# Pair values of a 27-wide Gram matrix taken along its diagonals: three row chunks in the first layer in place of four, one write per half tile, six reads

## The chip, the cores and the metric

The kernel runs on one core of a Trainium2 chip. The metric is the device time of one execution in microseconds (us), the median of 3 runs, taken without the profiler. In the rows PE is the matrix engine (PEld its weight load), DVE, ACT and POOL are the vector, scalar and GpSimd engines, and SPq, ACTq and POOLq are the queues on which SP, ACT and POOL issue transfers (DMAs).

## The reference

A batch of 512 rows looks up 27 embeddings of 128 numbers, takes the product of every pair of them, appends 16 dense features and runs three layers:

```python
e = jnp.stack([tbl_0[ids[:, 0]], ..., tbl_26[ids[:, 26]]], axis=1)   # 512 x 27 x 128
interactions = jnp.einsum('bnd,bmd->bnm', e, e)
i, j = jnp.triu_indices(27, k=1)
z = interactions[:, i, j]                                            # 512 x 351
h = jnp.concatenate([z, dense_ctx], axis=1)                          # 512 x 367
h = jnp.maximum(h @ W_top1 + b_top1, 0.0)                            # 367 x 512
h = jnp.maximum(h @ W_top2 + b_top2, 0.0)                            # 512 x 256
y = h @ W_top3                                                       # 256 x 1
```

Everything is float32.

## The kernel before

The batch is cut into T = 4 tiles of 128 rows. 15 features come by indirect gathers that POOL issues (L328, one for each feature and tile, and one more for the last tile, 61 in all). PE transposes them in groups of up to four ("quads", numbered 0 to 15, four for each tile, L347), and DVE or ACT copies them into `ET` (L479, L560). The other 12 features, from the smaller tables, are picked by products with a one-hot matrix `hot` (L369), which DVE and ACT build (L500, L586) while SP loads the tables. POOL holds back a gather at six places until DVE has built a certain `hot` (the list `HELD`, L326).

Then `product_unit` (L386) multiplies, for two batch rows at a time, the 27 features with themselves, eight units in all, two for each tile. DVE and ACT copy the results to `gram` (L513, L597). The Gram values lie there with one batch row to a group of partitions, while the first layer wants one pair to a partition. So each tile goes through HBM: SP writes one half and ACT the other, each in two DMAs (`write_last_block` L182, `write_other_blocks` L189), into `pair_blocks`, where each of three blocks holds 9 of the 27 columns. `read_pairs` (L210) reads it back into `zT`, with 128-byte pieces of 32 batch rows. In the blocks the pairs are rectangles, so 459 rows are read for 351 pairs; those of a pair that comes twice meet rows of zeros in the weights. With the 16 dense rows they fill NC = 4 chunks:

```python
CHUNKS = [[(2, 0, 14)], [(1, 0, 14)], [(0, 0, 8), (1, 14, 17)], [(2, 14, 26)]]   # (block, first row, end)
SP_READS = [(0, 1, 2), (0, 1, 2, 3), (0, 1, 2, 3), (0, 2)]                       # chunks by tile
ACT_READS = [(3,), (), (), (1,)]
```

For the last tile chunk 0 and 2 are read by SP, 1 by ACT and 3 by POOL. The first layer (L398 for tiles 1 and 2, which waits for all chunks first; L413 for tiles 0 and 3, which waits chunk by chunk) does four products of 128 columns for each chunk. Each float32 product stands as two records in the trace, so a chunk is 8 records and a layer 32.

The order of the work on PE, DVE and ACT is a list written out by hand, `steps`; each engine walks through it and does its part:

```python
steps = quads(9, 10) + units(0) + [("write", 0), ("unit", U)] + quads(10, 12) + [("unit", U + 1), ("read", 0), ("write", 1)]
steps += units(2) + [("write", 2)] + quads(12, 13) + mlp(0) + quads(13, 14)
steps += [("layer1", 1), ("layer3", 0), ("layer2", 1), ("layer2_end", 1)] + quads(14, 16) + [("layer3", 1)]
steps += units(3) + [("write", 3)]
```

After that come the three layers of tile 2 and those of tile 3. SP goes through the tiles in order: wait for the Gram matrix, write, wait for what was written, read.

## Time and profile before

| | us |
|---|---|
| median of 3 runs without the profiler | 112.94 (112.81 to 113.18) |
| span of the profiled execution | 141.2 |
| PE busy / PE weight load busy | 112.1 / 93.6 |
| DVE / ACT / POOL busy | 73.8 / 70.5 / 68.8 |

The profile gives the span of the execution that it recorded, from the first to the last instruction, and no time of that execution beside it: what lies around the span is not known. The span is 28.3 us longer than the median of the runs without the profiler, so this trace holds waits that those runs don't have, or have shorter. Times in the rows are in the trace's own coordinates, 0 to 141.2.

### The profile page before, as it was taken

How to read it: one execution, taken by the hardware profiler on the slowest of the kernel's cores; microseconds unless marked ns; L12 is line 12 of the kernel's file. 1: busy time of each engine (PE TensorE's matmuls, PEld its weight loads, DVE VectorE, ACT ScalarE, POOL GpSimd, SP SyncE). 2: the span in 40 equal slices, each digit the busy share in tenths (PEclk: the TensorE clock that was granted, in tenths of full speed). 3: DMA queues.
4: the chain of work that ended last, by engine and by line, in shares of the span. 5: the costliest groups of instructions: out<-in, count | busy, mean ns of one | idle time of the engine just before them, and what ended most of it. 6: DMA issues, size and time to landing. Idle time of an engine off the chain costs nothing.

```text
span 141.2 us, 2513 instructions
## 1 busy us (share of the span) xinstructions
PE 112.1 (79%) x1025; PEld 93.6 (66%) x1025; DVE 73.8 (52%) x68; ACT 70.5 (50%) x100; POOL 68.8 (49%) x81
## 2 busy tenths in 40 slices
PE   5969999998999987069994212126999999999894
PEld 5938777775877865047892110105999998899792
DVE  2799999999999980699100000200446212451221
ACT  4099999999999960699440000002255211151021
POOL 2578788887877887147877777740000000002000
PEclk9999999999999999965899555555599999999999
DMA  2896788989768699201112222110037543004300
GB/s 62 292 357 220 239 241 268 267 252 279 170 229 258 150 383 331 61 0 37 48 45 56 60 56 56 44 49 0 14 119 188 118 105 49 0 5 143 54 0 1
DMA packets 15877, 18.74 MB, mean 133 GB/s; under 512 B 9425, under 2 KB 11805, under 8 KB 15738
## 3 DMA queue, kind: packets, MB, share of 16 engines
q1 hardware_dynamic: 11864, 13.39, 32.1%
q0 software_dynamic: 2000, 4.06, 10.2%
q10 hardware_dynamic: 2002, 1.14, 2.8%
q8 instruction: 8, 0.13, 0.4%
q14 instruction: 3, 0.02, 0.0%
HBM read 16.80 MB, written 1.77 MB: 132 GB/s over the span
## 4 chain that ended last, share of the span: by engine, by line
PE 42%; DVE 31%; issue 18%; another core or an unknown queue 4%; DMA 3%; SPq 0%; ACT 0%; DVEq 0%
DVE hot L500 22%; PE psG L386 14%; DVE parts L505 9%; PE psG L369 7%; PE psG L413 5%; PE psH L398 5%; PE psH L429 4%; DMA pick_ids<-in_picked_ids 3%; PE psT L347 3%; PE psG L429 1%; PE psH L444 1%; DVE hot L488 1%; PE psG L444 0%; SPq L264 0%
## 5 line engine op out<-in xcount | busy, mean ns | idle before, releaser
L328 POOL DMA_INDIRECT rows<-in_tbl,ids_sb x61 | 62.9, 1032 | 19.7 <-issue 15.8
L369 PE MATMUL psG<-hot,parts 128*128 128x512 f32 (+1 forms) x216 | 56.1, 410 | 7.7 <-DVE hot L500 6.2
L369 PEld LDWEIGHTS psG<-hot,parts 128*128 128x128 f32 x216 | 40.7, 198 | 19.9 <-DVE hot L500 6.2
L500 DVE TENSOR_TENSOR hot<-pick_ids,psH 128x1536 fp32r<-128x1536 int32 (+2 forms) x23 | 41.6, 1851 | 5.3 <-remote 5.3
L386 PE MATMUL psG<-ET 128*52 128x54 f32 x512 | 20.2, 234 | 17.3 <-issue 17.3
L386 PEld LDWEIGHTS psG<-ET 128*52 128x52 f32 x512 | 17.5, 146 | 20.3 <-issue 19.7
L513 DVE COPY gram<-psG 128x432 f32<-128x432 f32 x8 | 7.2, 903 | 36.0 <-issue 21.3
L597 ACT COPY gram<-psG 128x432 f32<-128x432 f32 x8 | 7.2, 905 | 32.0 <-remote 23.2
L586 ACT ACTIVATE hot<-pick_ids,row_no 128x512 fp32r<-128x512 int32 (+1 forms) x30 | 19.4, 711 | 0.0
L210 POOL DMA_DIRECT2D zT<-pair_blocks x1 | 0.9, 883 | 35.9 <-DMA pair_blocks<-gram 35.9
L505 DVE TENSOR_TENSOR parts<-table,parts 128x1024 fp32r<-128x1024 f32 (+1 forms) x12 | 16.3, 1358 | 0.0
L590 ACT ACTIVATE hot<-hot 128x1024 fp32r<-128x1024 f32 (+2 forms) x12 | 15.0, 1247 | 0.4
L577 ACT CAST parts<-table 128x1280 fp32r<-128x1280 f32 (+1 forms) x11 | 12.8, 1167 | 0.0
L565 ACT COPY ET<-psG 128x512 f32<-128x512 f32 (+1 forms) x12 | 7.5, 622 | 10.0 <-remote 6.1
L560 ACT COPY ET<-psT 128x512 f32<-128x512 f32 (+1 forms) x13 | 7.3, 573 | 4.7 <-PE psT L347 4.7
L347 PE MATMUL psT<-ident,rows 128*128 128x128 f32 x61 | 8.9, 274 | 0.0
L347 PEld LDWEIGHTS psT<-ident,rows 128*128 128x128 f32 x61 | 7.2, 140 | 1.2
L413 PE MATMUL psG<-zT,w_sb 126*128 126x128 f32 (+2 forms) x64 | 7.7, 278 | 0.0
L413 PEld LDWEIGHTS psG<-zT,w_sb 126*128 126x128 f32 (+2 forms) x64 | 7.4, 191 | 0.3 <-issue 0.2
L398 PE MATMUL psH<-zT,w_sb 126*128 126x128 f32 (+2 forms) x64 | 7.6, 276 | 0.0
L398 PEld LDWEIGHTS psH<-zT,w_sb 126*128 126x128 f32 (+2 forms) x64 | 7.3, 191 | 0.1
L449 PE MATMUL psH<-ident 128*128 128x128 f32 x28 | 5.7, 397 | 1.5 <-POOL ident L303 1.5
(35 smaller groups left out, 47.0 us busy)
## 6 DMA issues: line engine op xcount, KB each, us to landing
table<-in_tbl SPq DMA_DIRECT2D x6, 640.0 KB
table<-in_tbl SPq DMA_DIRECT2D x6, 512.0 KB
pick_ids<-in_picked_ids SPq DMA_DIRECT2D x11, 256.0 KB, 3.3
w_sb<-in_w SPq DMA_DIRECT2D x1, 1024.0 KB
rows<-in_tbl,ids_sb POOLq DMA_INDIRECT x61
pair_blocks<-gram ACTq DMA_DIRECT2D x4, 144.0 KB, 2.5
pair_blocks<-gram SPq DMA_DIRECT2D x4, 144.0 KB, 3.5
w_sb<-in_w SPq DMA_DIRECT2D x1, 512.0 KB
```

Of the source, the lines that this page charges most:

```text
L328: pool.indirect_dma_start(out=rows[:, n % RING, x, :], out_offset=None, in_=gathered_tables[f], in_offset=bass.IndirectOffsetOnAxis(ap=ids ...
L347: last = pe.transpose(psT[:, n % 2, x, :], rows[:, n % RING, x, :], ident[:, :])
L369: last = pe.matmul(psP[:, k % 2, 0:looked_up(k)], parts[:, k % 2, x, c, :], hot[:, k % 2, c, 0:looked_up(k)], start=x == 0 and c == 0, sto ...
L386: last = pe.matmul(psG[R * h:R * h + S * J, m % 2, bank, S * F * x:S * F * (x + 1)], group[:, 0:S * J], group, start=True, stop=True)
L398: last = pe.matmul(h1_psum(t, n), w1_sb[0:ROWS[c], c, P * n:P * (n + 1)], zT[0:ROWS[c], t, c, :], start=c == 0, stop=c == NC - 1)
L413: last = pe.matmul(h1_psum(t, n), w1_sb[0:ROWS[c], c, P * n:P * (n + 1)], zT[0:ROWS[c], t, c, :], start=c == 0, stop=c == NC - 1)
L500: dve.tensor_tensor(hot[:, k % 2, first:end, 0:many], pick_ids[:, k % TABLES, 0:many].unsqueeze(1).to_broadcast(shape), numbers.unsqueeze( ...
L505: dve.tensor_tensor(parts[:, k % 2, 1, 0:CH[k], :], table[:, k % TABLES, 0:CH[k], :], parts[:, k % 2, 0, 0:CH[k], :], ALU.subtract).then_i ...
L565: act.copy(ET[:, 0:tiles, :, F - 1 - k, :], psP[:, k % 2, 0:P * tiles].rearrange("d (t s g) -> d t g s", t=tiles, s=S)).then_inc(picked_ou ...
L577: act.copy(parts[:, k % 2, 0, 0:CH[k], :], table[:, k % TABLES, 0:CH[k], :]).then_inc(high_ready, 1)
L586: act.activation(hot[:, k % 2, c, 0:looked_up(k)], pick_ids[:, k % TABLES, 0:looked_up(k)], ACT.Abs, bias=row_number(k, c), scale=-1.0).th ...
L590: act.activation(last, last, ACT.Relu, bias=1.0, scale=-1.0).then_inc(last_hot_ready, 1)
```

## The change

`gram` is written as it lies, all 27 columns of a half tile in one DMA (64 rows of 3,456 bytes, `write_gram`, L182 of the kernel after), into `pair_grams`. There the value of features i and j has the number 27 i + j. Since 27 i + j equals j - i plus a multiple of 28, all numbers 7 m + 1 lie on diagonals j - i of 1, 8, 15, 22 or their like below the main one, and no pair comes twice; the numbers 7 m + 1, 7 m + 2 and 7 m + 3 (104 each), 28 m + 7 (26) and 28 m + 14 (13) hold each of the 351 pairs once. `read_pairs` reads these with a stride, two DMAs for each chunk (104 and 13 rows), six for a tile in place of five. The 16 dense rows go to chunks 0 and 1, 8 each, by two DMAs. The chunks have 125, 125 and 117 rows, where the four had 126, 126, 99 and 124. `w1` is padded to 3 x 128 rows (768 KB) in place of 4 x 128 (1,024 KB). The left operand of a pair product takes all 54 columns in place of 52, since the strided numbers reach into the last feature's row.

```diff
-    J = F - 1
...
-    NB = F // WIDTH
...
-    PAIR_ROWS = [sum(WIDTH * (end - first) for b, first, end in chunk) for chunk in CHUNKS]
-    ROWS = PAIR_ROWS[:NC - 1] + [PAIR_ROWS[NC - 1] + DN]
+    PAIR_ROWS = [sum(end - first for step, offset, first, end in chunk) for chunk in CHUNKS]
+    DENSE_IN = 2
+    DH = DN // DENSE_IN
+    ROWS = [n + (DH if c < DENSE_IN else 0) for c, n in enumerate(PAIR_ROWS)]
...
-    SP_READS = [(0, 1, 2), (0, 1, 2, 3), (0, 1, 2, 3), (0, 2)]
-    ACT_READS = [(3,), (), (), (1,)]
+    SP_READS = [(0, 1), (0, 1, 2), (0, 1, 2), (0,)]
+    ACT_READS = [(2,), (), (), (1,)]
+    POOL_READS = (2,)
...
-        blocks = nc.dram_tensor("pair_blocks", (T, NB, S, G, WIDTH * GH), fp32, kind="Internal").ap()
+        grams = nc.dram_tensor("pair_grams", (T, S, G, F * GH), fp32, kind="Internal").ap()
...
-        def write_last_block(eng, t, s):
-
-            eng.dma_start(blocks[t, NB - 1, s, :, :],
-                          gram[s:P:S, t % 2, s, WIDTH * (NB - 1):F, :].rearrange("q j g -> q (j g)")
-                          ).then_inc(last_block_out[t], 16)
-
-        def write_other_blocks(eng, t, s):
-
-            src = gram[s:P:S, t % 2, s, 0:WIDTH * (NB - 1), :]
-            eng.dma_start(blocks[t, 0:NB - 1, s, :, :].rearrange("b q x -> q b x"),
-                          src.rearrange("q (b j) g -> q b (j g)", b=NB - 1)).then_inc(other_blocks_out[t], 16)
-
-        def wait_block_of(eng, t, c):
-
-            if CHUNKS[c][0][0] == NB - 1:
-                eng.wait_ge(last_block_out[t], 16 * S)
-            else:
-                eng.wait_ge(other_blocks_out[t], 16 * S)
+        def write_gram(eng, t, s):
+
+            eng.dma_start(grams[t, s, :, :], gram[s:P:S, t % 2, s, :, :].rearrange("q j g -> q (j g)")
+                          ).then_inc(gram_out[t], 16)
 
         def wait_written(eng, t):
 
-            eng.wait_ge(last_block_out[t], 16 * S)
-            eng.wait_ge(other_blocks_out[t], 16 * S)
+            eng.wait_ge(gram_out[t], 16 * S)
 
         def read_pairs(eng, t, c):
 
             r = 0
-            for b, first, end in CHUNKS[c]:
-                n = WIDTH * (end - first)
-                src = blocks[t, b, :, :, :].rearrange("s (h i) x -> (s h) i x", h=H)[:, first:end, :]
+            for step, offset, first, end in CHUNKS[c]:
+                n = end - first
+                src = grams[t, :, :, :].rearrange("s (h i) x -> (s h) (i x)", h=H)
+                src = src[:, 0:step * GH * end].rearrange("q (m k g) -> k m q g", k=step, g=GH)
                 eng.dma_start(zT[r:r + n, t, c, :].rearrange("r (q g) -> r q g", q=Q),
-                              src.rearrange("q i (j g) -> (i j) q g", g=GH)).then_inc(chunk_in[t][c], 16)
+                              src[offset, first:end, :, :]).then_inc(chunk_in[t][c], 16)
                 r += n
...
         steps += mlp(2) + [("read", T - 1), ("layer3", T - 2), ("chunk", 0), ("chunk", 1), ("chunk", 2),
-                           ("chunk", 3), ("relu1", T - 1), ("layer2", T - 1), ("layer3", T - 1)]
+                           ("relu1", T - 1), ("layer2", T - 1), ("layer3", T - 1)]
...
-            sp.dma_start(zT[PAIR_ROWS[NC - 1]:ROWS[NC - 1], :, NC - 1, :],
-                         dense_rows.rearrange("k (t p) -> k t p", p=P)).then_inc(dense_in, 16)
+            for c in range(DENSE_IN):
+                sp.dma_start(zT[PAIR_ROWS[c]:ROWS[c], :, c, :],
+                             dense_rows[DH * c:DH * (c + 1), :].rearrange("k (t p) -> k t p", p=P)).then_inc(dense_in, 16)
...
-                write_last_block(sp, t, 0)
-                write_other_blocks(sp, t, 0)
+                write_gram(sp, t, 0)
+                wait_written(sp, t)
                 for c in SP_READS[t]:
-                    wait_block_of(sp, t, c)
                     read_pairs(sp, t, c)
...
-            wait_block_of(pool, T - 1, 3)
-            read_pairs(pool, T - 1, 3)
+            wait_written(pool, T - 1)
+            for c in POOL_READS:
+                read_pairs(pool, T - 1, c)
...
-                            last = pe.matmul(psG[R * h:R * h + S * J, m % 2, bank, S * F * x:S * F * (x + 1)],
-                                             group[:, 0:S * J], group, start=True, stop=True)
+                            last = pe.matmul(psG[R * h:R * h + S * F, m % 2, bank, S * F * x:S * F * (x + 1)],
+                                             group, group, start=True, stop=True)
...
-                    pe.wait_ge(dense_in, 16)
+                    pe.wait_ge(dense_in, 16 * DENSE_IN)
...
-                write_last_block(act, t, 1)
-                write_other_blocks(act, t, 1)
+                write_gram(act, t, 1)
 
             def read_half(t):
+                wait_written(act, t)
                 for c in ACT_READS[t]:
-                    wait_block_of(act, t, c)
                     read_pairs(act, t, c)
...
-        return a * n - a * (a + 1) // 2 + b - a - 1 if i < j else -1
-
-    chunks = [[pair(i, j) for b, first, end in chunk for i in range(first, end)
-               for j in range(WIDTH * b, WIDTH * (b + 1))] for chunk in CHUNKS]
-    chunks[-1] += [n * (n - 1) // 2 + x for x in range(n_dense)]
+        return a * n - a * (a + 1) // 2 + b - a - 1
+
+    chunks = [[pair(*divmod(step * m + offset, n)) for step, offset, first, end in chunk for m in range(first, end)]
+              for chunk in CHUNKS]
+    for c in range(2):
+        chunks[c] += [n * (n - 1) // 2 + x for x in range(n_dense // 2 * c, n_dense // 2 * (c + 1))]
     return [c + [-1] * (128 - len(c)) for c in chunks]
...
 PICKED = 12
-WIDTH = 9
-CHUNKS = [[(2, 0, 14)], [(1, 0, 14)], [(0, 0, 8), (1, 14, 17)], [(2, 14, 26)]]
+CHUNKS = [[(7, 1, 0, 104), (28, 7, 0, 13)], [(7, 2, 0, 104), (28, 7, 13, 26)], [(7, 3, 0, 104), (28, 14, 0, 13)]]
```

On PE, from the units of tile 3 to the last tile's layer 1, these rows stood in the order of the program before (`zT` is the input of layer 1, `chunk_in_t_c` says that chunk c of tile t has landed):

```order
L386 MATMUL psG<-ET 52x54 [waits gram_act]
L386 MATMUL psG<-ET 52x54 x15
L398 MATMUL psH<-zT,w_sb 128x128 [waits chunk_in_2_3,chunk_in_2_2,y_ready,chunk_in_2_1,chunk_in_2_0]
L398 MATMUL psH<-zT,w_sb 128x128 x15
...
L413 MATMUL psG<-zT,w_sb 128x128 [waits chunk_in_3_2]
L413 MATMUL psG<-zT,w_sb 128x128 x3
L413 MATMUL psG<-zT,w_sb 128x128 [waits chunk_in_3_3]
L413 MATMUL psG<-zT,w_sb 128x128 x3
L429 MATMUL psH<-h,w_sb 128x128 [waits h1_dve]
```

and these stand there now:

```order
L373 MATMUL psG<-ET 54x54 [waits gram_act]
L373 MATMUL psG<-ET 54x54 x15
L385 MATMUL psH<-zT,w_sb 128x128 [waits chunk_in_2_2,y_ready,chunk_in_2_1,chunk_in_2_0]
L385 MATMUL psH<-zT,w_sb 128x128 x11
...
L400 MATMUL psG<-zT,w_sb 128x128 [waits chunk_in_3_2]
L400 MATMUL psG<-zT,w_sb 128x128 x3
L416 MATMUL psH<-h,w_sb 128x128 [waits h1_dve]
```

Four products, 8 records, are gone from each tile's layer 1, and nothing else moved on PE. On SP's queue these rows stood for tile 3 before:

```order
L182 DMA pair_blocks<-gram 64x288 [waits gram_act,gram_dve]
L189 DMA pair_blocks<-gram 64x2x288
L210 DMA zT<-pair_blocks 126x4x32 [waits last_block_out_3]
L210 DMA zT<-pair_blocks 72x4x32 [waits other_blocks_out_3]
L210 DMA zT<-pair_blocks 27x4x32
```

and these now:

```order
L182 DMA pair_grams<-gram 64x864 [waits gram_act,gram_dve]
L196 DMA zT<-pair_grams 104x4x32 [waits gram_out_3]
L196 DMA zT<-pair_grams 13x4x32
```

The first read no longer starts when a third of the tile is written: it waits for all of it. POOL's queue ended before with one read, and ends now with two, of the chunk that layer 1 takes last:

```order
L196 DMA zT<-pair_grams 104x4x32 [waits gram_out_3]
L196 DMA zT<-pair_grams 13x4x32
```

ACT reads chunk 1 of tile 3 and chunk 2 of tile 0, each with such a pair of rows in place of one.

## Rows read from the trace of the kernel before

**Rows 1.** The page: busy time by engine.

```profile
span 141.2 us, 2513 instructions
PE 112.1 (79%) x1025; PEld 93.6 (66%) x1025; DVE 73.8 (52%) x68; ACT 70.5 (50%) x100; POOL 68.8 (49%) x81
```

**Rows 2.** Stages: PE, PEld, DVE, ACT, POOL busy (instructions), granted clock, DMA share, GB/s.

```profile
52.50:57.70 5.20, 3.27 (x17) 2.48 (x15) 0.01 (x1) 0.00 (x0) 3.66 (x4) 1.00 0.91 290
...
73.40:97.10 23.70, 6.56 (x72) 4.19 (x71) 0.88 (x1) 0.80 (x2) 15.26 (x17) 0.60 0.18 48
```

**Rows 3.** Chain that ended last, in order of time: start, us, what.

```profile
52.51 5.21 another core or an unknown queue
...
61.82 6.99 PE psG L369 x17
...
125.92 3.77 PE psH L398 x32
```

**Rows 4.** Timeline, PE and POOL: start, us, operation, idle before it.

```profile
51.16 4.17 PE L369 MATMUL psG<-hot,parts 128*128 128x512 f32 x17 [0.42 <-DVE hot L500]
...
62.34 1.65 POOL L328 DMA_INDIRECT rows<-in_tbl,ids_sb  x1
...
66.80 1.52 POOL L328 DMA_INDIRECT rows<-in_tbl,ids_sb  x1 [0.30 <-issue]
...
92.59 0.94 POOL L328 DMA_INDIRECT rows<-in_tbl,ids_sb  x1 [0.30 <-issue]
...
97.08 5.48 PE L386 MATMUL psG<-ET 128*52 128x54 f32 x123 [0.37 <-issue]
...
103.41 4.88 PE L386 MATMUL psG<-ET 128*52 128x54 f32 x192
...
120.84 1.04 PE L347 MATMUL psT<-ident,rows 128*128 128x128 f32 x8
```

**Rows 5.** The same stages' view after the last gather's issue.

```profile
94.80:96.00 1.20, 0.56 (x2) 0.16 (x1) 0.00 (x0) 0.00 (x0) 0.00 (x0) 0.50 0.00 0
```

**Rows 6.** Groups by line and shape: count, busy us, mean ns, idle before.

```profile
L413 PE MATMUL psG<-zT,w_sb 126*128 126x128 f32 x32 | 4.1, 282 | 0.0
...
L413 PE MATMUL psG<-zT,w_sb 99*128 99x128 f32 x16 | 2.1, 275 | 0.0
```

**Rows 7.** Timeline, tiles 0 and 1 on SP's queue.

```profile
101.09 0.53 SPq L182 DMA_DIRECT2D pair_blocks<-gram  x1
...
104.84 1.85 SPq L210 DMA_DIRECT2D zT<-pair_blocks  x4
...
110.52 2.15 SPq L210 DMA_DIRECT2D zT<-pair_blocks  x5
```

**Rows 8.** Timeline, tile 3, all engines and queues.

```profile
126.06 0.91 ACT L597 COPY gram<-psG 128x432 f32<-128x432 f32 x1 [0.65 <-PE psG L386]
127.03 0.46 SPq L182 DMA_DIRECT2D pair_blocks<-gram  x1
...
129.16 1.73 SPq L210 DMA_DIRECT2D zT<-pair_blocks  x3
...
129.43 0.88 POOL L210 DMA_DIRECT2D zT<-pair_blocks  x1 [35.90 <-DMA pair_blocks<-gram]
...
130.18 0.35 ACTq L210 DMA_DIRECT2D zT<-pair_blocks  x1
...
132.85 3.65 PEld L413 LDWEIGHTS psG<-zT,w_sb 126*128 126x128 f32 x32 [0.22 <-issue]
```

**Rows 9.** POOL's read of tile 3, from issue to landing.

```profile
DMA to landing us min/median/max: 2.9/2.9/2.9
```

**Rows 10.** Windows while the reads of tile 3 land.

```profile
131.00:132.00 1.00, 0.79 (x8) 0.60 (x6) 0.17 (x1) 0.00 (x0) 0.00 (x0) 1.00 0.90 145
132.00:133.00 1.00, 0.68 (x5) 0.40 (x6) 0.48 (x3) 0.00 (x0) 0.00 (x0) 1.00 0.18 27
```

**Rows 11.** Windows while the weights load.

```profile
50.00:52.00 2.00, 1.58 (x8) 0.99 (x7) 2.00 (x2) 1.60 (x2) 1.69 (x3) 1.00 1.05 413
```

More of the change, by code:

```diff
@@ L166, in dlrm_tower @@
         gram_act = sem("gram_act")
-        last_block_out = [sem(f"last_block_out_{t}") for t in range(T)]
-        other_blocks_out = [sem(f"other_blocks_out_{t}") for t in range(T)]
+        gram_out = [sem(f"gram_out_{t}") for t in range(T)]
         chunk_in = [[sem(f"chunk_in_{t}_{c}") for c in range(NC)] for t in range(T)]
```

## Prediction

> **What bounds the kernel now.** I begin with the page's first rows: no engine is busy for the whole span, PE comes nearest with 79% [rows 1]. So the bound changes from stage to stage, and the windows and the chain that ended last have to say where. Two stages stand out. In one of 5.2 us DVE and ACT are idle while the DMA engines are at 0.91 of their time; the chain gives 5.21 us there to "another core or an unknown queue". In one of 23.7 us PE has 72 records at a mean granted clock of 0.60, between its two levels of 1.2 and 2.4 GHz [rows 2, 3]. The rows show no tile and no engine that it waits for. The runs without the profiler take 112.94 us, 28.3 less than the span, and these two stages are the only ones large enough to hold that. So I rebuild the time without them. The first three units and the transposes of quad 9 end at 102.56, after 29.1 us from 73.40; the same 192 records of the next three units took 4.88 us: 24.3 us less. The 5.2 us stall goes. After it, with PE just out of its idle time, 17 pick products took 6.99 us, where 17 had taken 4.17 before it: 2.8 us less. 141.2 - 24.3 - 5.2 - 2.8 = 108.9 [rows 2 to 4]. The median is 4.0 us above, which I count as what lies around the span. The sum below is one of differences, and I take them off the 112.94.
>
> In this rebuilt time two chains meet at quad 15, the last to be transposed. PE's own chain (picks, units, layers of tiles 0 and 1) reaches it, halfway through the eight transposes at 120.84, so at about 121.4 in the trace, and at 121.4 - 32.3 = 89.1 in the rebuilt time. POOL issues the last gather at 92.59, and the DMA engines are idle from 94.8 on. POOL was held up by the stall alone, since it waited for a `hot` of DVE's, so its data are there at 94.8 - 5.2 = 89.6, or 1.3 us sooner (88.3) if its two long issues (1.65 and 1.52 against 0.94) belong to the stall too [rows 4, 5]. That is even within a microsecond, so work that PE loses before quad 15 may be worth nothing. Behind quad 15 PE is the chain: units of tile 3, layer 1 of tile 2, layer 1 of tile 3, with no wait for a transfer in the rows; the weight load is idle for 0.22 us ahead of the last layer 1 [rows 8].
>
> **The change, part by part.**
>
> *Four products, 8 records, less in each layer 1.* A layer of 32 records takes 3.77 us, so a chunk is 3.77 / 4 = 0.94 us. That the chunk holds fewer or more rows doesn't matter: records of 99 rows take 275 ns, of 126 rows 282 [rows 3, 6]. So -0.94 for each of four tiles: two after quad 15 (-1.88) and two ahead of it (-1.88 at most).
>
> *54 columns in place of 52 on the left.* 192 records in 4.88 us are 25.4 ns each [rows 4]. No row has 54 columns. Lower bound 0 (the 54 columns that stream by are the same), upper bound in proportion, 25.4 x 2/52 = 1.0 ns: 0.13 us for the 128 records after quad 15, 0.38 for the 384 ahead. I take the upper ones, since weight loads fill this stage as much as products do.
>
> The Trainium skill (TensorE: Matmul & The Clock Gate, LDWEIGHTS) says that a weight load takes its columns divided by 1.2 ns, whatever the number of rows. By that a left operand of 54 costs 1.7 ns more than one of 52, an estimate of 0.21 us after quad 15 in place of 0.13, and the sum would be 0.08 us less gain. On the number of rows the trace agrees (275 against 282 ns).
>
> *Ahead of quad 15.* PE gains at most 1.88 - 0.38 = 1.5 us there. The other bound is 0, if the gathers come at 89.6 or later. The rows put PE between 0.5 us ahead of the data and 0.8 behind (89.1 against 89.6 and 88.3). Such slack, plus an error of half a microsecond in a rebuilt time, is what can be gained; I take 0.6 us. Tile 1's reads could bind first: SP issues six reads there in place of five, at 2.15 / 5 = 0.43 each, while the write is one issue of about 0.5 in place of two, and so the last read goes out at about the same time, against a PE that comes 0.94 sooner [rows 7]. That stays inside the 0.6.
>
> *The write, tile 3.* Before, `gram` was ready at 126.97, SP issued at 127.03, the smaller write was seen landed at 129.16 (2.1 us), and both at 130.18 (3.15 us), of which the second issue cost 0.5 [rows 8]. Now one DMA holds all. No row shows a write of 3,456 bytes a row. Lower bound 2.1, as the smaller write; upper bound 3.75, as tile 0 had it (101.09 to 104.84) [rows 7]. I take 2.6, the full one without the second issue: all written at 129.65.
>
> *The reads, tile 3.* SP's second read for chunk 0 goes out 0.43 later, at 130.1. What a read takes on SP's queue is not in a row of its own. POOL's took 2.9, with 0.88 of issue; SP had issued its last by 130.89, and the DMA share falls from 0.90 to 0.18 after 132 [rows 8 to 10]. So the estimate is 1.5 to 2.5; I take 2.0: chunk 0 is in at 132.1. PE, 0.94 sooner, wants it at 132.85 - 0.94 = 131.9. So it waits 0.2, where it waited for nothing. Chunk 1 (ACT, the same times) is wanted 0.94 later. Chunk 2 is POOL's now, by two reads: 129.65, then 0.88 of issue and the 0.30 that lies between POOL's issues, and from 130.83 another 2.9: 133.7. It is wanted at 132.1 + 1.88 = 134.0. So it is just hidden, and 0.3 later it isn't. Behind POOL's reads nothing is queued; ACT's two reads stand ahead of its activations of tile 3, which can't come before the layer 1 that starts at 132.85 has done its last chunk, and cost nothing while that cover of more than 2 us lasts.
>
> *The rest.* `w1` is 256 KB smaller. At 413 GB/s [rows 11] that is 0.6 us less of transfer in the stage of full DMA. In the rebuilt time nothing waits there, so 0; if the 5.2 us stall hangs on those transfers and is partly there without the profiler, up to -0.6. One more small DMA for the dense rows is issued on SP long ahead of its use: 0.
>
> Sum: -1.88 + 0.13 + 0.2 - 0.6 = -2.15, and 112.94 - 2.15 = **110.8 us**.
>
> The Trainium skill (DMA: Bandwidth & Descriptors, Rules for kernel authors) speaks against this side of the change: many small transfers should be one large one, since under 64 KB one pays mostly overhead. All the new reads are under that, and there is one more in a tile. The trace shows the overhead as issue time, 0.43 us a read; by the rule, the second read of a chunk costs as much issue as the first, and with that the sum comes out at the same 2.15 us.
>
> **The rivals.** *(A) The gathers don't bind.* Then all that is gained ahead of quad 15 counts: -1.88 + 0.13 + 0.2 - 1.5 = -3.05: 109.9, and with the smaller `w1` 109.3. For it: the order of `steps` puts quads 14 and 15 as late as it can, and the rebuilt slack may be short by a microsecond. Against it: POOL issues without a pause to the end, and the numbers meet.
>
> *(B) The exchange of tile 3 becomes the bound.* If the write takes 3.75, it has landed at 130.78, chunk 0 is in at 133.2 and PE waits 1.3 us in place of 0.2; POOL's last chunk then comes at 134.9, against a want of 135.1, so nothing is added. The gain is 1.88 - 0.13 - 1.3 = 0.45 us and what was gained ahead, 0.6: 111.9. For it: tiles 0 and 1 show such slow writes. Against it: tile 3's was fast, with no other traffic beside it.
>
> *(C) The strided reads are slow: no gain, or slower.* A 104-row read takes every seventh 128-byte piece, where the blocks gave 9 in a row. The old pieces filled a window at 0.90 share and 145 GB/s; a tile's 351 x 512 bytes = 180 KB at 145 / 0.9 = 161 GB/s take 1.1 us [rows 10]. At three times the time for a piece the reads end 2.2 us later; the wait of 0.2 becomes 2.4, tile 1's reads bind too and nothing is gained ahead: -1.88 + 0.13 + 2.4 = +0.65: 113.6. The point from which it decides is a wait of 1.75 us. For it: nothing in the rows shows a strided read. Against it: the pieces are as long as before, and 24% fewer.
>
> **How the numbers follow.** The forecast has 0.52, (A) 0.24, (B) 0.14, (C) 0.10. The likeliest case has its own range: 0 to 1.2 us ahead of quad 15 and a wait of 0 to 0.7 give 110.0 to 111.9. The range goes to both neighbours, down to (A) with the smaller `w1` and up past (B): 109.3 to 112.1. 0.3% is 0.34 us, about what a measurement of this kernel can tell from no change. (C) is shared between same and slower; a small part of (B) lies in "same": faster 0.87, same 0.06, slower 0.07.
>
> **What the profile after would show.** Layer 1 has 24 records in place of 32 and takes 2.8 us. The pair products have 54 columns and 192 records take 4.9 to 5.1 us. In tile 3 the first read is issued 2.6 us after the write, and PE is idle for 0.4 us or less ahead of the last layer 1. POOL's two reads start about 1.2 us apart and PE doesn't wait for chunk 2. If the slow stage of the units is there again, the gathers have landed long before quad 15, so the trace itself may show up to 3 us from quad 9 to the end where the runs without the profiler gain 2. An idle PE ahead of L400 of a microsecond or more is (B) or (C), told apart by when the first read is issued. Gains near 3 us in the runs are (A). What would make the prediction wrong above all is the rebuilt time: that the gathers and PE meet at quad 15 is worked out, not seen.

## The result and the profile after

The kernel after takes 111.98 us (median of 12 runs, 111.23 to 112.3), the kernel before 113.02 beside it (12 runs, 111.94 to 114.38): a ratio of 0.9914 (0.9887 to 0.9941), 0.97 us less (0.7 to 1.3). Ratios, here and below, leave disturbed executions out, so they differ somewhat from the quotient of the medians where these scatter, and the three profiles that are of such executions have a * in the tables. The direction is as forecast and the time lies in the range, near its upper end and just above the 110.0 to 111.9 of the likeliest case, but the gain is less than half of the 2.15 forecast. The profiled execution of the kernel after took 111.96 us with a span of 109.8, so 2.2 us lie around the span.

The page of the kernel after, its span, busy times, granted clock by slice and chain:

```profile
span 109.8 us, 2437 instructions
PE 99.7 (91%) x993; PEld 84.2 (77%) x993; DVE 73.7 (67%) x68; ACT 70.5 (64%) x100; POOL 69.1 (63%) x82
...
PEclk9999999999999999999999999999999999999999
...
POOL 37%; DVE 24%; issue 14%; DMA 12%; PE 9%; ACT 1%; SPq 1%; POOLq 0%; ACTq 0%
```

Neither of the two stages of [rows 2] is here. They are no work of the profiler's, as the prediction had it: of the five chips used below, three gave the kernel before 112.7 to 112.9 us without the profiler, and two 143.2 to 143.3. Each chip was used once, so the runs don't tell whether it is the chip or the hour; "of the first kind" and "of the second kind" below mean no more than these two times. So a clean trace of the kernel before is needed, and one taken on a chip of the first kind (span 110.4) stands here. From its PE timeline, the units on (start, us, operation, idle before it):

```profile
65.53 4.88 PE L386 MATMUL psG<-ET 128*52 128x54 f32 x192
70.34 0.98 PE L347 MATMUL psT<-ident,rows 128*128 128x128 f32 x7
71.25 4.88 PE L386 MATMUL psG<-ET 128*52 128x54 f32 x192
76.06 0.66 PE L347 MATMUL psT<-ident,rows 128*128 128x128 f32 x4
77.99 3.81 PE L413 MATMUL psG<-zT,w_sb 126*128 126x128 f32 x32 [1.27 <-DMA zT<-pair_blocks]
...
83.96 3.74 PE L398 MATMUL psH<-zT,w_sb 126*128 126x128 f32 x32
...
90.04 1.04 PE L347 MATMUL psT<-ident,rows 128*128 128x128 f32 x8
91.01 0.60 PE L444 MATMUL psH<-h,w_sb 128*1 128x128 f32 x4
91.80 3.32 PE L386 MATMUL psG<-ET 128*52 128x54 f32 x128 [0.20 <-issue]
95.06 3.84 PE L398 MATMUL psH<-zT,w_sb 126*128 126x128 f32 x32
...
102.05 3.84 PE L413 MATMUL psG<-zT,w_sb 126*128 126x128 f32 x32
...
107.66 0.91 PE L444 MATMUL psH<-h,w_sb 128*1 128x128 f32 x4
```

The same view of the kernel after:

```profile
65.31 5.12 PE L373 MATMUL psG<-ET 128*54 128x54 f32 x192
...
71.27 3.05 PE L373 MATMUL psG<-ET 128*54 128x54 f32 x113
75.28 2.21 PE L373 MATMUL psG<-ET 128*54 128x54 f32 x79 [0.95 <-issue]
...
77.91 2.92 PE L400 MATMUL psG<-zT,w_sb 125*128 125x128 f32 x24
...
84.26 2.92 PE L385 MATMUL psH<-zT,w_sb 125*128 125x128 f32 x24 [1.10 <-DMA zT<-pair_grams]
...
89.53 0.60 PE L334 MATMUL psT<-ident,rows 128*128 128x128 f32 x4
91.19 0.66 PE L334 MATMUL psT<-ident,rows 128*128 128x128 f32 x4 [1.07 <-DMA rows<-in_tbl,ids_sb]
91.78 0.60 PE L431 MATMUL psH<-h,w_sb 128*1 128x128 f32 x4
92.57 3.41 PE L373 MATMUL psG<-ET 128*54 128x54 f32 x128 [0.20 <-issue]
95.91 2.94 PE L385 MATMUL psH<-zT,w_sb 125*128 125x128 f32 x24
...
102.30 2.94 PE L400 MATMUL psG<-zT,w_sb 125*128 125x128 f32 x24 [0.21 <-DMA zT<-pair_grams]
...
107.01 0.91 PE L431 MATMUL psH<-h,w_sb 128*1 128x128 f32 x4
```

The transposes of quad 15 are followed by the third layer of tile 1 (L444, now L431), so its start is the mark between the two parts of the prediction's sum. *Behind* it, to the start of the last third layer: 107.66 - 91.01 = 16.65 before, 107.01 - 91.78 = 15.23 after, so -1.42, where the prediction's terms gave -1.55. *Ahead* of it PE comes 0.77 us later, where 0.6 less was forecast, though both first layers there are 0.9 us shorter. The rows say where that went: 0.95 us in the middle of the second 192 records, for which the view names nothing ("issue"), 1.10 for tile 1's reads, 1.07 for the last gather. The kernel before shows one such wait, 1.27 for tile 0's reads. One pair of traces is no measure of the head, as will be seen; from the medians, 0.97 less in all and 1.42 less behind leave **+0.45 us ahead of quad 15** (0.1 to 0.8).

SP's queue in the kernel after, to set against [rows 7] and [rows 8]:

```profile
69.84 0.53 SPq L182 DMA_DIRECT2D pair_grams<-gram  x1
72.80 1.78 SPq L196 DMA_DIRECT2D zT<-pair_grams  x4
74.68 0.49 SPq L182 DMA_DIRECT2D pair_grams<-gram  x1
79.51 2.70 SPq L196 DMA_DIRECT2D zT<-pair_grams  x6
...
97.08 0.46 SPq L182 DMA_DIRECT2D pair_grams<-gram  x1
99.81 0.80 SPq L196 DMA_DIRECT2D zT<-pair_grams  x2
```

and the pieces of its chain behind the picks that are transfers (start, us, what):

```profile
87.28 3.86 DMA rows<-in_tbl,ids_sb
...
97.09 2.70 DMA pair_grams<-gram
...
100.15 2.10 DMA zT<-pair_grams
```

Tile 3 is as forecast: write 2.7 us (2.6), read 2.1 (2.0), a wait of 0.21 (0.2), none for POOL's chunk. But for tile 0 it is 3.0 us from the same write to the first read, and for tile 1 4.8: its six reads are in so late that PE waits. And the last gather lands 3.86 us after its issue.

### The profile page after: what moved, and what is told of

It reads as the page before. It is cut to its first block, busy times and chain, and to the rows that moved or that the text cites. A ratio compares the mean times of both kernels' runs of the same rounds, so it can differ in the third digit from the quotient of the medians.

```text
span 109.8 us, 2437 instructions
## 1 busy us (share of the span) xinstructions
PE 99.7 (91%) x993; PEld 84.2 (77%) x993; DVE 73.7 (67%) x68; ACT 70.5 (64%) x100; POOL 69.1 (63%) x82
## 4 chain that ended last, share of the span: by engine, by line
POOL 37%; DVE 24%; issue 14%; DMA 12%; PE 9%; ACT 1%; SPq 1%; POOLq 0%; ACTq 0%
POOL rows L314 35%; DVE hot L487 17%; DVE parts L492 6%; DMA pick_ids<-in_picked_ids 4%; DMA rows<-in_tbl,ids_sb 4%; PE psG L373 3%; PE psG L400 3%; DMA pair_grams<-gram 2%; POOL pause L300 2%; DMA zT<-pair_grams 2%; PE psH L416 2%; DVE hot L475 1%; PE psH L431 1%; ACT gram L584 1%; PE psT L334 1%
## 5 line engine op out<-in xcount | busy, mean ns | idle before, releaser
L356 PE MATMUL psG<-hot,parts 128*128 128x512 f32 (+1 forms) x216 | 53.2, 396 | 2.5 <-ACT hot L577 1.2
L356 PEld LDWEIGHTS psG<-hot,parts 128*128 128x128 f32 x216 | 38.7, 188 | 13.5 <-DVE hot L487 4.9
L373 PE MATMUL psG<-ET 128*54 128x54 f32 x512 | 13.8, 214 | 1.2 <-issue 1.2
L373 PEld LDWEIGHTS psG<-ET 128*54 128x54 f32 x512 | 13.4, 130 | 1.8 <-issue 1.8
L196 POOL DMA_DIRECT2D zT<-pair_grams x2 | 1.4, 727 | 11.9 <-DMA pair_grams<-gram 11.9
L436 PE MATMUL psH<-ident 128*128 128x128 f32 x28 | 6.2, 423 | 1.5 <-POOL ident L289 1.5
L436 PEld LDWEIGHTS psH<-ident 128*128 128x128 f32 x28 | 6.0, 332 | 1.5 <-POOL ident L289 1.5
L385 PE MATMUL psH<-zT,w_sb 125*128 125x128 f32 (+1 forms) x48 | 5.9, 278 | 1.1 <-DMA zT<-pair_grams 1.1
L385 PEld LDWEIGHTS psH<-zT,w_sb 125*128 125x128 f32 (+1 forms) x48 | 5.5, 191 | 1.4 <-issue 1.3
L416 PE MATMUL psH<-h,w_sb 128*128 128x128 f32 x48 | 6.3, 281 | 0.0
```

What stands on the lines that cost most here:

```text
L356: last = pe.matmul(psP[:, k % 2, 0:looked_up(k)], parts[:, k % 2, x, c, :], hot[:, k % 2, c, 0:looked_up(k)], start=x == 0 and c == 0, sto ...
L373: last = pe.matmul(psG[R * h:R * h + S * F, m % 2, bank, S * F * x:S * F * (x + 1)], group, group, start=True, stop=True)
L385: last = pe.matmul(h1_psum(t, n), w1_sb[0:ROWS[c], c, P * n:P * (n + 1)], zT[0:ROWS[c], t, c, :], start=c == 0, stop=c == NC - 1)
L416: last = pe.matmul(h2_psum(t, n), w2_sb[:, k, P * n:P * (n + 1)], h1[:, k, :], start=k == first, stop=k == end)
L436: pe.matmul(psH[:, 0, 0, :], ident[:, :], ident[:, :], start=True, stop=True)
```

## The experiments

Each ran beside runs of the kernel before on its own chip, and its ratio is to those. From exchange_only on, "theory W" in what was expected says that waits for transfers give the head's saving back, "theory P" that PE alone sets the time, so that its saving counts everywhere. "Head" means from the first units to the start of tile 1's third layer, "behind" from there to the start of the last third layer.

### Instructions shifted: is the late gather an accident of PE's instruction stream?

PE's instructions come by DMA too. The page of the kernel after has them in its section on DMA queues:

```profile
q8 instruction: 8, 0.13, 0.5%
```

Eight packets of 16 KB. The first theory, F, was that one of them stands ahead of the last gather on its DMA engine in the kernel after alone, so that a shift of PE's stream gives the microsecond back. The shift was made behind the third pick:

```diff
+                if x == 3:
+                    for y in range(8):
+                        pe.matmul(psH[:, 0, 0, 0:2], ident[:, :], ident[:, 0:2], start=True, stop=True)
```

The kernel before, unchanged: 

> The kernel before, unchanged, for a profile without the two stalls. Theory F (fetch): in the kernel after, the last gather lands 3.86 us after its issue because one DMA engine is busy for 1.1 us with 16 KB of PE's instructions just ahead of it; here the fetch falls elsewhere, the last gather lands in 2.4 to 2.8 us, and quad 15's transposes start at 90.0 to 90.7, against 91.19. Theory R (reads): the reads of tile 2 beside the last gathers delay it in both kernels; then the last gather lands 3.5 us or more after its issue here too. Theory P: PE comes so late in the kernel before (after 91) that gathers do not bind at all; then there is no wait for rows here. Time: 113.0 in all.

The kernel after with 8 such products: 

> The kernel after with 8 tiny matmuls (32 instructions, all into a part of psH that nothing reads) among the pick products, where PE has slack. They move every later fetch of PE's instructions about 32 instructions, some 1.9 us of layer work, earlier. Theory F: the last gather lands in 2.4 to 2.8 us and not 3.86, quad 15 starts at about 90.1, and the time is 0.8 to 1.1 us below the kernel after (111.0). Theory R: nothing changes, 112.0. If the moved fetch hits another gather or a read of tile 1 instead, the trace shows which.

With 16: 

> The same with 16 tiny matmuls (64 instructions): the fetch falls some 3.8 us earlier. Theory F: the last gather lands in 2.4 to 2.8 us and the time is again 0.8 to 1.1 us below the kernel after. Theory R: 112.0.

The kernel before with 8: 

> The kernel before with the 8 tiny matmuls. Theory F: the fetch moves by 32 instructions here as well, from about where it is in the padded kernel after to some 1.9 us earlier; the time stays at 113.0 within 0.4 us unless the fetch now meets a gather or a read. Theory R: 113.0.

| | us | ratio |
|---|---|---|
| before_again | 112.72 | 0.9995 (0.9958 to 1.0032) |
| after_pad8 | 112.45 | 0.9942 (0.9902 to 0.9981) |
| after_pad16 | 115.8 | 1.0233 (1.0179 to 1.0288) |
| before_pad8 | 113.6 | 1.0048 (1.0013 to 1.0083) |

The kernel before repeats within 0.05%. F's forecast missed: no pad gained. But the test isn't clean, since the pads held up the work itself: the units start at 66.11 with 8 of them (65.31 without) and at 69.53 with 16. What it did show: with 8 pads the gather is waited for no more, and PE waits 1.82 us for tile 0's reads instead, issued 4.9 us after the write. The loss in the head moves between transfers.

With 8 pads something else comes in, the granted clock. Behind that wait tile 0's layer of 24 records takes 4.54 us, where it takes 2.92 in the kernel after:

```profile
79.84 4.54 PE L400 MATMUL psG<-zT,w_sb 125*128 125x128 f32 x24 [1.82 <-DMA zT<-pair_grams]
```

The mean granted clock in these 4.54 us is 0.62, between the two levels of 1.2 and 2.4 GHz, and 1.00 before and behind them. So the wait cost 1.82 us and then 1.6 more. In the kernel after, where the waits are 0.95 to 1.10 us, the clock stays at 1.00, and behind the 1.42 of after_pad16 as well.

The trace holds each DMA packet with its start and length, which no view lists, and these records do show F's collision in the kernel after. One packet of PE's instructions runs from 88.84 to 89.97. All 4 KB pieces of the last gather start by 89.27 but one, which starts at 89.97, as if it stood behind that packet on one DMA engine; without it the gather would have been in some 0.9 us sooner. The clean trace of the kernel before has no such packet near its last gather, which lands in 2.4 to 2.7 us.

The same packets explain the break of 0.95 us. It comes after record 113 in the kernel after, and with 8 pads, which are 16 records, after record 97 (0.20 us). And in all six traces with a break (table below) PE goes on 1.3 to 1.5 us after the fourth packet has landed: at 75.28 after 73.93, or at 74.82 after 73.39 with 8 pads. So PE had run out of instructions. Where that packet is in earlier (72.43 in the clean trace of the kernel before, 72.67 in hold_off3*) there is no break.

The fourth packet is due just when tile 0's write goes out, at 70 to 73. If it comes behind the write (72.8 to 73.0 in three traces of the new exchange), PE starves. If it comes first, the write pays: with 8 pads it lands at 73.39, 120 of the write's 128 pieces are in by 73.1, and the others follow one by one from 73.37 on, the last at 74.81.

### Both halves apart: the exchange without PE's saving

Spare products of the size of the chunk that went (four of 128 columns, 8 records, into a part of PSUM that nobody reads) give PE its old work back, with the new exchange left as it is:

```diff
+            def spare_product(t, n):
+                pe.matmul(psH[:, 0, 0, :] if t == T - 1 else psH[:, 1, 2, :], w1_sb[0:ROWS[0], 0, P * n:P * (n + 1)],
+                          zT[0:ROWS[0], t, 0, :], start=True, stop=True)
+
...
+                if t in (0, 1, 2, 3):
+                    for n in range(N1):
+                        spare_product(t, n)
```

`exchange_only` has them in all four tiles, `spare_behind` in tiles 2 and 3 alone. `hold_off` takes the last of the places at which POOL holds back a gather out (`HELD` one shorter), and `warm10` has 10 products in place of 14 that warm PE up at the start.

exchange_only: 

> The kernel after, with four products of 128 columns more in each layer 1, whose results nothing reads, so that PE works as long as in the kernel before and only the exchange, the smaller w1 and the 54 columns differ. Theory W (two waits give the head saving back: tile 1's reads and the last gather): 0.2 us less than the variant with the extra products in tiles 2 and 3 alone plus at most 0.3, so 113.2 to 114.0. Theory P (PE's saving counts everywhere): 1.9 us more than that variant, 115 or more.

spare_behind: 

> The same with the extra products in tiles 2 and 3 alone, both behind quad 15. Both theories: the kernel after plus 1.88 less the 0.2 us that PE waits for tile 3's reads, 113.6 to 113.8. If it is under 113.2, PE was not the chain behind quad 15 either.

hold_off: 

> The kernel after without the last of the six places where POOL stops for DVE, so that the last 20 gathers are issued 0.55 us sooner. Theory W: the time falls by 0.5 us (the gather still takes 3.9 us to land) or by up to 1.07 (it slips past the fetch of instructions and lands in 2.4), 110.9 to 111.5. Theory P: 112.0.

warm10: 

> The kernel after with 10 warm-up products in place of 14 at the start: 16 instructions fewer, so each later fetch of PE's instructions comes 16 instructions later. Theory F: the fetch that met the last gather moves about 1 us past it, the gather lands in 2.4 to 2.8 us, quad 15 starts at 90.2 and the time falls by up to 1.0 us, 111.0 to 111.5. If the landing stays near 3.9 us with the fetch elsewhere, theory F falls. Fewer warm-up products may leave the first picks slower; then the start of the units moves from 65.31.

The chip of these four took 143.27 us for the kernel before: exchange_only 146.28, 1.0206 (1.0131 to 1.0281); spare_behind 144.67, 1.0131 (1.0047 to 1.0215); hold_off 142.79, 0.9964 (0.992 to 1.0009); warm10 143.09, 1.0043 (0.9991 to 1.0095). Their gathers landed long before quad 15 (the last is issued at 94.6 or sooner, the quad comes past 120), so they say nothing on the meeting of the two chains. But they say that the late exchange needs no gathers beside it. In all four PE waits for tile 0's reads, 0.9 to 1.6 us, which the kernel before doesn't on such a chip, and the DMA records show the same collision: a packet of instructions between 103.7 and 105.6, nine tenths of the write in by 105.5, its last piece at 106.3 to 106.7. The first two and hold_off were run again, with hold_off3, which takes three places out:

```diff
-    HELD = range(21, 21 + 4 * (FP - SHORT), 4)
+    HELD = range(21, 21 + 4 * (FP - SHORT - 3), 4)
```

exchange_only again: 

> Once more, for a chip on which the kernel before takes 113 us and not 143: PE works as long as in the kernel before, only the exchange, the smaller w1 and the 54 columns differ. Theory W (tile 1's reads and the last gather give the head saving back): up to 0.5 us above the variant with extra products behind quad 15 alone. Theory P (PE's saving counts everywhere): 1.9 us above it.

spare_behind again: 

> Once more: extra products behind quad 15 alone. Both theories: the kernel after plus 1.7 to 1.9 us, a ratio to the kernel before of 1.006 to 1.008.

hold_off again: 

> Once more: the last of POOL's six stops is gone, so the last 20 gathers go out 0.55 us sooner. Theory W: 0.5 to 1.07 us below the kernel after, a ratio to the kernel before of 0.982 to 0.987. Theory P: as the kernel after, 0.991.

hold_off3: 

> The last three of POOL's stops are gone, so the last gather goes out up to 1.65 us sooner and can't be what quad 15 waits for, even if it takes 3.9 us to land. Theory W: PE doesn't wait at quad 15, 1.07 us below the kernel after, a ratio of 0.982, unless the sooner gathers slow the picks. Theory P: 0.991.

| before 112.88 us | us | ratio | behind |
|---|---|---|---|
| exchange_only_b | 114.14 | 1.0079 (1.0036 to 1.0122) | 16.75 |
| spare_behind_b | 113.34 | 1.002 (0.9976 to 1.0063) | 16.75 |
| hold_off_b*, 6 runs | 111.54 | 0.9862 (0.9806 to 0.9919) | 15.42 |
| hold_off3*, 6 runs | 112.26 | 0.9862 (0.978 to 0.9945) | 15.20 |

With PE's work as before, the new exchange costs 0.79% = 0.9 us (0.4 to 1.4). Behind quad 15 that is 16.75 - 16.65 = 0.10, the 54 columns; so 0.8 (0.3 to 1.3) lies ahead, 0.26 of it again the 54 columns (5.01 in place of 4.88 for each 192 records, where nothing breaks them). Spares behind quad 15 cost 1.0020 / 0.9914 = 1.1%, 1.2 us, where the rows have 16.75 - 15.23 = 1.52; the ratio is somewhat below the 1.006 to 1.008 expected, but its interval meets them. Spares ahead of it cost 1.0079 / 1.0020 = 0.6%, 0.7 us (0 to 1.4) of the 1.88 that the records take. That is nearer theory W (up to 0.5) than P (1.9). So by these ratios the head pays 0.8 and gets back 0.7 of its 1.88; by the +0.45 of the medians it gets 0.35 back. Two lines of spare_behind_b, whose head is that of the kernel after:

```profile
75.37 2.21 PE L373 MATMUL psG<-ET 128*54 128x54 f32 x79 [0.96 <-issue]
...
90.22 0.66 PE L334 MATMUL psT<-ident,rows 128*128 128x128 f32 x4 [1.36 <-DMA rows<-in_tbl,ids_sb]
```

Here the reads of tile 1 were in time, PE stood at quad 15 by 88.87, and the gathers still bound. hold_off_b and hold_off3 have the lowest ratios, but their intervals meet that of the kernel after (0.9887 to 0.9941), so that they beat it isn't shown; hold_off3's rests on two executions. hold_off3*'s SP queue has a write of tile 0 that is read 5.2 us later:

```profile
69.81 0.53 SPq L182 DMA_DIRECT2D pair_grams<-gram  x1
74.98 2.81 SPq L196 DMA_DIRECT2D zT<-pair_grams  x4
```

### The head without an exchange, and the write in two

`two_writes` cuts the write in two DMAs, as the kernel before had it, and every wait counts both; `two_writes_hold_off` has the shorter `HELD` as well; `before_hold_off` is the kernel before with it. In `no_exchange_head` tiles 0 and 1 have no writes and no reads: `zT` is filled for them from a weight table at the start, so their output isn't the reference's.

```diff
+            for first, end in ((18, F), (0, 18)):
+                eng.dma_start(grams[t, s, :, GH * first:GH * end],
+                              gram[s:P:S, t % 2, s, first:end, :].rearrange("q j g -> q (j g)")
+                              ).then_inc(gram_out[t], 16)
```

```diff
+            for t in range(2):
+                for c in range(NC):
+                    sp.dma_start(zT[0:PAIR_ROWS[c], t, c, :], w2[0:PAIR_ROWS[c], 0:P]).then_inc(chunk_in[t][c], 16)
...
+                if t < 2:
+                    continue
                 write_gram(sp, t, 0)
```

two_writes: 

> The kernel after with each half tile written by two DMAs again (columns 18 to 26 first, then 0 to 17, in pieces of 1,152 and 2,304 bytes to a row), waited for together. Theory S (size: on one DMA engine the long pieces of the single write stand ahead of PE's 16 KB of instructions, and PE starves for 0.95 us in the units): the wait of 0.95 us inside the units of tiles 1 and 2 goes or shrinks, the tail loses 0.3 to 0.5 us by the second issue; in sum within 0.5 us of the kernel after, 0.988 to 0.996 to the kernel before. Theory C (which of the two comes first is chance, whatever their size): the wait is there again in the profile or tile 0's reads come later, and the time is the same or up to 0.5 us more.

before_hold_off: 

> The kernel before without the last of POOL's six stops. In its profile the last gather had landed before PE came to quad 15. Theory W says that gathers then bind little there: within 0.3 us of the kernel before, 0.997 to 1.003, where the same edit took 0.6 us off the kernel after. If it gains 0.5 us or more here too, the gathers bind in both and the gain of the edit says nothing about the change.

no_exchange_head: 

> The kernel after with no exchange for tiles 0 and 1: their Gram values aren't written or read, and their rows of zT are filled early with numbers from a weight table, so what comes out for those two tiles is not the reference's. PE's work is the same. Theory W: without the writes and reads of the head PE has no wait for them and doesn't starve in the units; quad 15 then starts when the last gather lands, at 89.7 to 90.2 in place of 91.19, and the time is 1.0 to 1.6 us below the kernel after, 0.977 to 0.983. Theory P: PE and the gathers alone set the head, 0.991.

two_writes_hold_off: 

> Both edits, two writes and the last stop left out: if theory S holds, the fastest so far, 0.980 to 0.986; if theory C holds, as the kernel with the last stop left out, 0.986.

This chip was of the second kind (before 143.21): two_writes 145.91, 1.0177 (0.9983 to 1.0372); before_hold_off 143.01, with no ratio on record; no_exchange_head 141.66, 1.0018 (0.9968 to 1.0068); two_writes_hold_off 143.1, 1.0121 (0.9991 to 1.025). None of these times decides the question. But no_exchange_head shows what the slow stage is not. Its windows (as [rows 2]) over both stages:

```profile
52.50:57.70 5.20, 3.58 (x18) 2.60 (x16) 0.14 (x1) 0.00 (x0) 3.79 (x4) 1.00 1.05 274
73.40:98.70 25.30, 7.66 (x83) 5.23 (x81) 0.88 (x1) 1.53 (x3) 16.65 (x18) 0.59 0.19 50
```

PE does 83 records in 25.3 us at a mean granted clock of 0.59 with no exchange under way at all. So the exchange isn't what holds it up. Behind that stage the trace gives PE's saving when nothing waits: from the second 192 records to tile 1's third layer 120.85 - 104.16 = 16.69 us, where [rows 4] give 121.80 - 103.41 = 18.39 (quads 14 and 15 end 0.96 after 120.84). That is -1.70, the two chunks' -1.80 and 0.13 for the 54 columns to 0.03.

The head without an exchange and the earlier gathers were then run on a chip of the first kind (before 112.68):

no_exchange_head again: 

> Once more, for a chip on which the kernel before takes 113 us: no exchange for tiles 0 and 1, whose rows of zT are filled early with numbers from a weight table, so that the output of those two tiles is not the reference's. Theory W: quad 15 starts when the last gather lands, at 89.7 to 90.2, and the time is 1.0 to 1.6 us below the kernel after, a ratio to the kernel before of 0.977 to 0.983. Theory P: 0.991.

before_hold_off again: 

> Once more: the kernel before without the last of POOL's six stops. Theory W: 0.997 to 1.003, since PE came to quad 15 after the last gather there. If it is 0.995 or less, the gathers bind in the kernel before too.

no_exchange_head_b took 111.52 us, 0.9865 (0.9819 to 0.991); before_hold_off_b 113.48, 0.9979 (0.9931 to 1.0028): by the ratio the earlier gathers change nothing measurable in the kernel before. PE's timeline of no_exchange_head_b:

```profile
71.05 5.01 PE L378 MATMUL psG<-ET 128*54 128x54 f32 x192
...
76.48 2.94 PE L405 MATMUL psG<-zT,w_sb 125*128 125x128 f32 x24
...
86.78 0.60 PE L339 MATMUL psT<-ident,rows 128*128 128x128 f32 x4
89.73 0.66 PE L339 MATMUL psT<-ident,rows 128*128 128x128 f32 x4 [2.36 <-DMA rows<-in_tbl,ids_sb]
90.32 0.60 PE L436 MATMUL psH<-h,w_sb 128*1 128x128 f32 x4
```

This is the floor of the head. PE is at quad 15 by 87.4 and waits 2.36 us for the last gather, which POOL issued at 87.22. All that a perfect exchange could give is 91.01 - 90.32 = 0.69 us by these two traces. By the ratio it is less: 1.35% is 1.52 us in all, of which 1.42 behind, so 0.1 (-0.4 to 0.6) ahead. But its 12 executions are of two sorts. Four, the profiled one among them, have a mean granted clock of 1.00 and took 110.2 to 110.7; eight have 0.984 or 0.985, as after_pad8 has in the profiled execution, and took 111.5 to 112.4. None of the 23 executions of the kernel before beside them is under 0.999. The four lie at 0.979 on average, inside the 0.977 to 0.983 expected, 2.3 us below the kernel before and so 0.9 ahead of quad 15. The other eight lose about 1.5 us on average, near the 1.6 that the lower clock cost in after_pad8; where it fell in them isn't seen, as none was profiled. So an exchange taken away doesn't give all it could, because PE then waits longer for the last gather and in most executions has the lower clock. In the comparison that counts, the kernel after has 0.984 or 0.985 in 3 of 12 executions, and they are no longer than the others (111.70 to 112.23).

All profiles of the 113-us kind beside each other (us; behind is to the start of the last third layer; "issue" is the break for lack of instructions):

| | units start | PE's waits in the head | tile 0's write to first read | third layer of tile 1 | behind |
|---|---|---|---|---|---|
| before_again | 65.53 | 1.27 reads 0 | 3.8 | 91.01 | 16.65 |
| before_pad8 | 66.14 | 0.54 reads 0, 1.08 reads 1 | 4.0 | 92.66 | 16.66 |
| before_hold_off_b* | 65.66 | 1.29 issue, 0.59 reads 1 | 2.4 | 92.66 | 16.65 |
| exchange_only_b | 65.20 | 0.95 issue, 0.43 reads 1 | 3.9 | 91.50 | 16.75 |
| spare_behind_b | 65.28 | 0.96 issue, 1.36 gather | 3.0 | 90.81 | 16.75 |
| after | 65.31 | 0.95 issue, 1.10 reads 1, 1.07 gather | 3.0 | 91.78 | 15.23 |
| after_pad8 | 66.11 | 0.20 issue, 1.82 reads 0 | 4.9 | 92.65 | 15.17 |
| hold_off_b* | 65.16 | 0.91 issue, 2.08 reads 0 | 5.7 | 92.83 | 15.42 |
| hold_off3* | 65.27 | 1.89 and 0.36 reads 0 | 5.2 | 92.14 | 15.20 |
| after_pad16 | 69.53 | 1.42 reads 0, 1.34 reads 1 | 4.3 | 95.47 | 15.22 |
| no_exchange_head_b | 65.20 | 2.36 gather | none | 90.32 | 15.21 |

The last column falls in two groups and nothing else. The third layer of tile 1 starts 1.7 us apart within the three traces of the kernel before and 2.0 apart within those of the new exchange (after_pad16 aside). What scatters is when transfers land and, in after_pad8, hold_off_b* and hold_off3*, the clock: tile 0's layer takes 1.6 to 1.8 us longer there behind its wait. With the * rows left out, the write of tile 0 is read 3.0 to 4.9 us later with the new exchange and 3.8 to 4.0 in the kernel before.

## Why the prediction was right and where it was wrong

**Right: the mechanism behind quad 15.** Each term was measured near its size, from start to start in the two timelines. A layer of three chunks is 0.90 us shorter (3.84 to 2.94), so two of them -1.80 (-1.88). The 54 columns cost 3.41 - 3.32 = 0.09 for 128 records (0.13, the upper bound, was taken, and 0.21 was the prediction's other estimate). The wait of 0.2 came as 0.21, from a write of 2.7 and a read of 2.1 us, and 0.08 more around it, as the layer now starts 0.81 after the layer ahead of it and before 0.52. POOL's chunk was hidden. That is -1.80 + 0.09 + 0.29 = -1.42, against -1.55. The time came out in the predicted range because this part, two thirds of the sum, held, and because the range reached past rival (B).

**Wrong: the step "Ahead of quad 15", "I take 0.6 us".** It came out at +0.45 (0.1 to 0.8), 1.05 us off, which is nearly all of the 1.2 between forecast and result. The slack itself was sized about right. The two chains did meet there, as the prediction said: in the clean trace of the kernel before the last gather goes out at 87.54 and lands 2.4 to 2.7 us later, so by 90.2, and PE starts on quad 15 at about 90.5. The head without any exchange gains 0.69 us by traces and 0.9 by the executions whose clock stays at 1.00.

What failed is the sentence on tile 1's reads, "That stays inside the 0.6". It counted the issues on SP's queue, took for granted that write and reads land as fast as before, and put PE's own instructions at nothing. With PE's work held as before, the change costs the head 0.8 us (0.3 to 1.3). PE would come 0.9 sooner to tile 1's layer, and 1.8 sooner to quad 15; the transfers don't. So PE waits: in the five profiles of the new exchange without a * twice for tile 0's reads, three times for tile 1's and twice for the gather, and in three of them 0.95 us for instructions, which neither profile of the kernel before without a * has to. The bound of 3.75 from [rows 7] was applied to tile 3 in rival B; where it belonged was tiles 0 and 1, from whose rows it was read. The prediction also put the smaller `w1` at nothing; the units start at 65.2 to 65.3 in the unpadded kernels with it and at 65.5 in the clean trace of the kernel before, which may be its gain, but with 8 pads the two starts are the same, so it isn't shown.

**Wrong, without a price: what the long trace was.** The prediction took the 28.3 us for waits of the profiled execution. They belong to runs on chips of the second kind, with or without the profiler. Leaving them out was right all the same, since the traces of 113-us chips lack both stages. The rebuilt trace had PE start its units at 73.43 in the old coordinates, 65.4 in the new with the 8.0 of stall and slow picks taken off; in the clean trace they start at 65.53. PE was to be at quad 15 at 89.1; it was there at about 90.5, for the most part through the wait of 1.27 us for tile 0's reads, which the slow trace doesn't have. Of the two times for the last gather's data 89.6 was the better, since POOL's two long issues (1.65 and 1.52 us) are in the trace of the kernel after too and don't belong to the stall. And 2.1 us lie around the span (112.45 us for the execution of span 110.4), not 4.0.

**The rivals.** (A), that the gathers don't bind and all that is saved ahead counts, is out by the time; the gathers bind in two of the seven traces with the new exchange and in the one without. (B) and (C) are out for tile 3: the write landed in 2.7 us and strided reads in 2.0 to 2.6, as this view of the kernel after gives for those of the 24 whose landing it can tell:

```profile
DMA to landing us min/median/max: 2.0/2.3/2.6
```

The Trainium skill (DMA: Bandwidth & Descriptors, Rules for kernel authors) counsels against many small transfers, and the prediction set one more read at its issue time, 0.43 us. Behind quad 15 the trace agrees with that way of pricing: SP's first read goes out at 99.81 and the chain goes on through its second at 100.15, 0.34 later, and no more.

**Open.** That transfers in the head collide with PE's instruction packets is shown packet by packet, though that they share one DMA engine is read from their times alone. How much of the 0.8 us is due to it, and why the new exchange pays more than the old, isn't: in the kernel before the write of tile 0 meets the fourth packet too (71.19 to 72.43; the write's last piece is in at 74.01). That one long write is worse than two shorter ones isn't shown, and the kernel that would tell, two_writes, ran on a 143-us chip alone; what holds PE up there for 25 us no run tells.

## What to carry to other kernels

Where two chains meet, work taken off one is worth the slack and not a microsecond more, while the same work taken off behind the meeting counts in full: here 1.42 of 1.88 us against nothing. Price an exchange through HBM at each place it stands, from rows of that place, and against a consumer that comes sooner by what is saved: the exchange of tile 3, with no instruction packet beside its write, was read after 2.7 us, those of tiles 0 and 1 met such packets. A wait can cost more than its length, if the granted clock falls behind it. And when the trace's span and the median differ by a quarter, look first for executions of another kind, and read the head from several traces before trusting one.

## What the runs showed of the hardware

The same program took 112.7 to 112.9 us on three chips and 143.2 to 143.3 on two, each used once. On the latter PE got 72 records in 23.7 us (kernel before) or 83 in 25.3 (no exchange in the head) at a granted clock of 0.60 and 0.59, and the view names nothing that it waited for.

PE's instructions come in eight packets of 16 KB, 0.9 to 1.7 us each. One that is late stops PE (0.9 to 1.3 us in five traces), and one that is in time can hold back a piece of another transfer to its own end: of the last gather in the kernel after (3.86 us from issue to landing, 2.4 to 2.7 without), or of tile 0's write with 8 pads.

Behind a wait of 1.82 us the granted clock fell, to a mean of 0.62 over the next 4.54 us, at a cost of 1.6; behind waits of 1.07, 1.10 and 1.42 us in other traces, and behind the one of 2.36 in no_exchange_head_b, it stayed at 1.00.

And one and the same write of 216 KB in the head was read back 3.0 to 4.9 us after its issue, 2.7 us for tile 3. The Trainium skill (DMA: Bandwidth & Descriptors, Anatomy of one DMA) gives a DMA about 2.0 us fixed and its bytes at 436 GB/s, by which 216 KB take 2.5 us, an estimate from a fit that the page made for GpSimd's path. Tile 3's write agrees with it; the head's do not.
